# One cross-attention and expert kernel: token scaling on GpSimd, and four merges around it

## What is computed

```
ln   = layer_norm(x) * ln_w + ln_b                 # per token
xq_j = fp8(bf16(clip(ln / in_scale_j)))            # j = q, qx, k, v: four scalings of the same tokens
q    = LN(xq_q @ wq) * qln_w + qln_b               # LN over each head's 128 columns; k likewise, v without LN
core = softmax(q k^T / sqrt(128)) v                # 8 groups, 2 heads each, 64 keys
xout = the same with qx, and with kx, vx from the context
catq = fp8(bf16(clip([core, xout] / proj_smooth)))
x    = x + catq @ wproj * scale
x    = x + experts(layer_norm(x))                  # 8 experts, top 2, and a shared one
```

## Time and profile before

| | us |
|---|---|
| median of 3 runs | 955.73 |
| lowest, highest | 955.66, 956.96 |
| the profiled execution | 956.31 |
| its span | 954.5 |

### The profile page before, as it was taken

The page is one execution under the profiler, slowest core; times in us unless marked ns, Lnnn a source line. Parts: engine busy times, 40 slices in busy tenths (PEclk is TensorE's granted clock), DMA queues, the critical chain, the costliest instruction groups (busy, mean ns, idle before and its releaser), DMA issues.

```text
span 954.5 us, 23599 instructions
## 1 busy us (share of the span) xinstructions
PE 916.9 (96%) x8264; PEld 621.1 (65%) x8264; DVE 793.8 (83%) x1720; ACT 735.6 (77%) x1370; POOL 454.5 (48%) x673
## 2 busy tenths in 40 slices
PE   5688999999999999999999999999999999999997
PEld 3365666766767676766767667666655566666665
DVE  6889999999999999999999999987998744444443
ACT  5998899899899899899999999864656545555554
POOL 5335656465565555555555555531056513333333
PEclk9989999999999999999999999999999999999999
DMA  9933201001001001001100100213558713333323
GB/s 215 333 90 70 64 24 51 30 30 44 29 30 46 29 29 46 29 30 31 44 30 24 52 29 24 102 44 117 178 157 262 249 48 54 51 74 51 46 32 37
DMA packets 36754, 70.48 MB, mean 74 GB/s; under 512 B 3616, under 2 KB 24736, under 8 KB 36512
## 3 DMA queue, kind: packets, MB, share of 16 engines
q1 hardware_dynamic: 27184, 54.39, 17.5%
q0 software_dynamic: 9456, 14.59, 9.1%
HBM read 55.52 MB, written 18.68 MB: 78 GB/s over the span
## 4 chain that ended last, share of the span: by engine, by line
PE 64%; DVE 21%; issue 7%; ACT 5%; POOL 1%; DMA 1%; DVEq 0%; POOLq 0%; ACTq 0%
PE b_pj L346 17%; PE b_tr L362 7%; PE b_pj L1339 5%; PE b_o L403 5%; PE b_o L1374 5%; PE b_sc L374 4%; PE b_acc L446 4%; PE b_o L1466 3%; PE b_tr L1339 3%; DVE ssq L526 3%; PE b_sc L1339 3%; DVE nrm L537 3%; PE b_pj L1419 2%; DVE cat L578 2%; PE b_pt L1363 2%
## 5 line engine op out<-in xcount | busy, mean ns | idle before, releaser
L700 POOL TENSOR_TENSOR root<-vareps,neghalf 128x4 f32<-128x4 f32 (+1 forms) x128 | 173.8, 1358 | 10.0
L693 POOL TENSOR_TENSOR var<-ssq,unit 128x4 f32<-128x4 f32 (+1 forms) x128 | 54.3, 424 | 235.1 <-DVE ssq L526 235.1
L346 PE MATMUL b_pj<-w_hi,xq 128*128 128x512 f16 x384 | 148.9, 388 | 1.1 <-DVE xq L682 0.8
L346 PE MATMUL b_pj<-w_lo,xq 128*128 128x512 f16 x384 | 148.3, 386 | 0.0
L526 DVE TENSOR_REDUCE ssq<-sq 128x4 f32<-128x512 f32 x192 | 130.3, 679 | 3.3 <-ACT sq L458 2.1
L537 DVE TENSOR_TENSOR nrm<-raw,rstd 128x512 f32<-128x512 f32 x192 | 128.8, 671 | 4.2 <-POOL rstd L704 3.5
L362 PE MATMUL b_tr<-ident,nrm 128*128 128x128 f32 x768 | 120.5, 280 | 11.6 <-DVE nrm L537 7.0
L458 ACT ACTIVATE sq<-b_pj 128x512 f32<-128x512 f32 x192 | 114.2, 595 | 18.2 <-PE b_pj L346 14.7
L1315 POOL DMA_INDIRECT out<-xn x39 | 60.6, 1553 | 136.2 <-ACT xn L1545 110.5
L362 PEld LDWEIGHTS b_tr<-ident,nrm 128*128 128x128 f32 x768 | 87.7, 141 | 48.3 <-DVE nrm L537 18.1
L468 ACT ACTIVATE raw<-b_pj 128x512 f32<-128x512 f32 x192 | 116.0, 604 | 0.0
(11 more groups left out here) (327 smaller groups left out, 2271.7 us busy)
## 6 DMA issues: line engine op xcount, KB each, us to landing
nst<-in_ffw SPq DMA_DIRECT2D x40, 512.0 KB, 3.3
wload<-in_ffw SPq DMA_DIRECT2D x20, 512.0 KB, 4.5
xbuf<-zero SPq DMA_DIRECT2D x13, 387.0 KB, 9.6
xn<-xbuf SPq DMA_DIRECT2D x9, 516.0 KB, 3.7
x_sb<-in_x SPq DMA_DIRECT2D x4, 512.0 KB, 14.1
wproj<-in_ctxT SPq DMA_DIRECT2D x1, 2048.0 KB, 10.9
xhl<-in_w_all SPq DMA_DIRECT2D x4, 512.0 KB, 18.2
wproj<-in_wprojT POOLq DMA_DIRECT2D x4, 512.0 KB, 5.0
```

Source lines behind the costliest of these rows:

```text
L346: last = pe.matmul(o, x, w[kind][:, k, at:at + BANK], start=(k == 0 and n_ == 0), stop=(k == KT - 1 and n_ == len(terms) - 1))
L700: pool.tensor_tensor(root[:, r % 2, c, :], vareps[:, r % 2, c, :], neghalf[:, 0:1].unsqueeze(2).to_broadcast(shape), ALU.pow).then_inc(s[" ...
```

## The change

Five edits.

1. From tile 2 on, the four scalings of a tile are one GpSimd product `y16 = lnT * rin` of 128x1024 elements with both inputs in SBUF. It stands behind both rstd chains and the rows in GpSimd's list, in the second of the four iterations of a tile. ScalarE's eight instructions for that tile go. `y16` now holds all four parts.
2. VectorE clips and rounds a tile's tokens in two instructions of 128x1024 instead of eight of 128x256, in the third of the four iterations.
3. The rstd chain is two instructions: one with a multiply and an add, and the power. The factor `unit` moves into the eviction's scale, as `hw = weight * unit`, two small VectorE instructions at the start.
4. `b_o0` and `b_o1` are one tensor `b_oo`, and `cat` is one instruction over both banks (128x1024).
5. The squares of banks 1 and 2 are summed in one instruction, behind `cat`; `sq` has three buffers instead of two.

```diff
             def act_square(c):
-                    after(act, "ssq_done", m - 1)
-                    act.activation(sq[:, m % 2, :], b_pj[c % 2][:, :], ACT.Square)
+                    after(act, "ssq_done", 2 * N if c else 2 * N - 1)
+                    act.activation(sq[:, c, :], b_pj[c % 2][:, :], ACT.Square)
...
+            def pool_token_scaled(pool, t, part):
+                if part != 1:
+                    return
+                pool.wait_ge(s["lnt_done"], KT * t + KT)
+                pool.wait_ge(s["q16_done"], scaled(t))
+                pool.tensor_tensor(y16[:, :, :, :], lnT[:, :, :].unsqueeze(2).to_broadcast([P, KT, 4, P]),
+                                   rin[:, :, :].rearrange("p j k -> p k j").unsqueeze(3).to_broadcast([P, KT, 4, P]),
+                                   ALU.mult).then_inc(s["y_done"], 1)
...
             def dve_quantize(dve, t, part):
+                if t >= 2 and part != 2:
+                    return
+                j = slice(0, 4) if t >= 2 else PARTS[part]
...
-                last = dve.tensor_tensor(cat16[:, :, b * S:(b + 1) * S], ...    # for b in range(2)
+                dve.tensor_tensor(cat16[:, :, :].rearrange("p a (b s) -> p b a s", s=S),
+                                  b_oo[:, :, :].rearrange("p b (a s) -> p b a s", s=S), smooth, ALU.mult)
...
             def pool_rstd(q):
-                    pool.tensor_tensor(var, ssq, unit2, ALU.mult)
-                    pool.tensor_tensor(vareps, var, epsc, ALU.add)
-                    pool.tensor_tensor(root, vareps, neghalf, ALU.pow)
-                    pool.tensor_tensor(rstd, root, unit, ALU.mult)
+                    pool.tensor_scalar(vareps, ssq, unit2[:, j:j + 1], EPS, ALU.mult, ALU.add)
+                    pool.tensor_tensor(rstd, vareps, neghalf, ALU.pow)
...
-                    (PREP, act_token_scaled, "tokens"),
...
-                    (3, dve_squares(0), "squares 0"),
+                    (3, dve_squares(0, 1), "squares 0"),
                     (1, dve_sum, "sum"),
-                    (3, dve_squares(1), "squares 1"),
                     (-1, dve_cat, "cat"),
-                    (3, dve_squares(2), "squares 2"),
+                    (3, dve_squares(1, NN), "squares 1"),
...
-                run_slots(pool, [(3, pool_rstd(0)), (3, pool_rstd(1)), (ROWS, pool_rows)],
+                run_slots(pool, [(3, pool_rstd(0)), (3, pool_rstd(1)), (ROWS, pool_rows), (PREP, pool_token_scaled)],
```

More of the change, by code:

```diff
@@ L205, in build @@
             b_sc = bank("b_sc", banks)
-            b_o = [bank(f"b_o{n}", banks) for n in range(2)]
+            b_oo = banks.enter_context(nc.psum_tensor("b_oo", [P, 2, BANK], F32))
+            b_o = [b_oo[:, n, :] for n in range(2)]
             b_acc = bank("b_acc", banks)
@@ L576, in dve_cat @@
                 after(dve, "clip_done", N)
[L577 to L581, removed]
+                smooth = wide(rsm[:, r * n:(r + 1) * n], S).unsqueeze(1).to_broadcast([P, 2, n, S])
+                dve.tensor_tensor(cat16[:, :, :].rearrange("p a (b s) -> p b a s", s=S),
+                                  b_oo[:, :, :].rearrange("p b (a s) -> p b a s", s=S), smooth, ALU.mult)\
+                    .then_inc(s["cev_done"], 1)
             def dve_clip(dve, N):
@@ L634, in act_token @@
                 act.wait_ge(s["tr_done"], t + 1)
-                after(act, "y_done", 4 * t)
+                after(act, "y_done", scaled(t))
                 for k in range(KT):
@@ L691, in step @@
                     shape = [P, (NN - 1) if q else 1, HC]
[L692 to L698, removed]
+                    pool.wait_ge(s["ssq_done"], 2 * N + (2 if q else 1))
+                    pool.tensor_scalar(vareps[:, r % 2, c, :], ssq[:, r % 2, c, :], unit2[:, j:j + 1], EPS,
+                                       ALU.mult, ALU.add).then_inc(s["pool_ve"], 1)
                     pool.wait_ge(s["pool_ve"], e)
-                    pool.tensor_tensor(root[:, r % 2, c, :], vareps[:, r % 2, c, :],
-                                       neghalf[:, 0:1].unsqueeze(2).to_broadcast(shape), ALU.pow).then_inc(s["pool_pw"], 1)
-                    pool.wait_ge(s["pool_pw"], e)
                     after(pool, "norm_done", NN * (N - 2) + (NN if q else 1))
-                    pool.tensor_tensor(rstd[:, r % 2, c, :], root[:, r % 2, c, :],
-                                       unit[:, j:j + 1].unsqueeze(2).to_broadcast(shape), ALU.mult)\
+                    pool.tensor_tensor(rstd[:, r % 2, c, :], vareps[:, r % 2, c, :],
+                                       neghalf[:, 0:1].unsqueeze(2).to_broadcast(shape), ALU.pow)\
                         .then_inc(s["rs_done"], 1)
@@ L860, in attention_scalar @@
                     (-2, "raw 3"): lambda: high(2, 4),
-                    (-2, "token"): lambda: (high(2, 5), squares(0)),
-                    (-2, "tokens"): lambda: (squares(1), high(3, 2), squares(2)),
+                    (-2, "token"): lambda: (high(2, 5), squares(0), squares(1), high(3, 2), squares(2)),
                     (-2, "rows"): lambda: (high(3, 3), squares(3)),
@@ L1592, in _ @@
                 for n in range(2, 6):
[L1593 removed]
+                    tail[FIRST - 2 + n, "token"] = shared(n)
                 attention_scalar(act, tail)
```

59 lines of the change are left out of this document (32 added, 27 removed).

## The result

The changed kernel takes 972.19 us (median of 4 runs, 970.95 to 976.32) against 955.72: a ratio of 1.0177 with the interval 1.0164 to 1.0191. It is slower by 16.5 us; the forecast was 947 and its range ended at 972.

What follows compares the result with a forecast made beforehand. TensorE was taken as full in the regular attention, late behind VectorE by 2%, with a ceiling near 19 us; 956.3 - 7.2 - 2.0 - 0.5 + 0.2 = 946.8, stated as 947 us, range 943 to 972.

Steps and rivals of the forecast that it cites:

- The step that failed: GpSimd's product beside VectorE's nrm: VectorE's loss put at nothing; the other end was the product's whole length.
- the second half of such an instruction holds nobody: Read from L720, GpSimd's 256 elements of 1.23 us: a nrm begun in its middle took 0.69 us, no more than others.
- Rival 1: GpSimd's product holds the critical nrm: 1.6 us in each of 14 tiles, +22, less 6 gained, 972; chance 0.33.
- a gain of 6 us: In rival 1, what remains of the gain from the first stretch and a part of the waits: -6 us.
- Rival 2: nrm starts first, the product holds bank 2's nrm: TensorE loses some 0.5 us per tile; 953 to 956; chance 0.14.
- The waits of 9.6 us: Transposes' weight loads waiting for nrm, 110 to 600 us: ceiling 9.6 us there, three quarters to go, -7.2 us.
- That floor: Regular stretch: behind the waits for nrm TensorE's own instructions follow one another, so relieving other engines gives no more.
- rival 3: TensorE is full already: 3 to 4 of the 9.6 us go at most, 951 to 954; chance 0.11.
- The chain: GpSimd's rstd chain for banks 1 and 2: no fourth step, rstd ready at 313.74 instead of 314.37, 0.63 us earlier.
- The first slots: First 110 us, seven to eight slots with VectorE late: -2 us, bounds 0 and -5, of 8.0 us of waits.
- the place of the joined sums: VectorE's merged sums of squares: their place costs nothing, as the chain for banks 1 and 2 already waited for both.
- ScalarE's saved time: Eight instructions, 3.1 us per tile, go: worth nothing in the regular stretch, some tenths in the first slots; ScalarE near 85%.

Runs made afterwards that it cites:

- e8: The changed kernel with the GpSimd product replaced by a multiply of one tensor with one factor per partition, same place and size; 956.17 us in one run.
- e3: The changed kernel with the GpSimd product moved ahead of bank 0's rstd, waiting for the iteration's last nrm (bank 2); 955.80 us, ratio 0.9998 to the kernel before.
- e9: The changed kernel with the product one iteration later, ahead of bank 0's rstd, waiting only for bank 1's nrm; 957.06 us, ratio 1.0000 to the kernel before.
- e7: e3 with edit 5 undone (sums of squares of banks 1 and 2 apart again); 952.28 us, ratio 0.9948 to the kernel before.
- e1: The changed kernel with edits 1 and 2 undone, ScalarE writing the scaled tokens again; 960.67 us, ratio 1.0044 to the kernel before.
- e5: The kernel before with edit 3 alone, the shorter rstd chain; 956.60 us, ratio 1.0000 to the kernel before.
- e6: The kernel before with edit 5 alone, the joined sums of squares; 960.54 us, ratio 1.0051 to the kernel before.
- e11: The kernel before with edits 1 and 2 only, the product placed as in e3; 957.56 us, ratio 1.0012 to the kernel before.

## Why the prediction was wrong

**The step that failed** is the one that put VectorE's loss at nothing, on the earlier trace rows; measured, the held `nrm` costs 1.1 us in each of 14 tiles, 15.7 us. The rows were true: a `nrm` begun 0.62 us into GpSimd's 256 elements was not held. What I made of them was not. I took "the second half of such an instruction holds nobody" for a price of the whole product, though the `nrm` at stake begins 0.1 to 0.2 us behind the product, in its first part, which those rows do not show. e8 shows what they did show: a GpSimd instruction of one tensor and factors per partition lets VectorE go long before it ends. A product with two inputs holds it almost to its end: 1.90 us, and `nrm` ends 0.55 us behind it.

The Trainium skill (SBUF — State Buffer, Who interferes with whom) had named the mechanism, and this trace agrees with it on the product (0.69 us became 2.38). I set its rule aside with one counterexample; the counterexample narrowed the rule and did not refute it. Where the Trainium skill (SBUF — State Buffer, Terms) has the shared ports "held for the full instruction", e8 disagrees: 3.38 us long, and a two-input `nrm` that began inside it ended 1.2 us before it did. The 4497 ns that the Trainium skill (GPSIMD Engine Reference, section 3.1) gives for 2048 elements are of an add; half of it, an estimate of 2.25 us, is above the 1.90 measured for this product.

**Rival 1** was the right one. Its product of 2.5 us was 1.90, its `nrm` came 0.07 us behind the product where 0.1 to 0.2 was worked out, and the stall by its own formula is then 1.0 us per tile; measured is 37.41 against 36.29 per four in e3, 1.12 us per tile, 15.7 us over 14. It named 972 us, and that it met 972.19 is partly luck: two errors of some 6 us cancel. The stall was 22 us and is 16, and it counted a gain of 6 us where e3, with nobody held, has none (955.80); with a product of 1.9 us it would have said some 964. **Rival 2** did not come about, as `nrm` stood behind the product. Its cost was tried as e9: held in the second place, the norm costs nothing in the regular stretch, where I had put 0.5 us.

**The waits of 9.6 us** were mis-sized as a ceiling. They are waits of the weight loads, which idle beside running matmuls. The matmuls' own wait for `nrm` is a line of its own in the view of the earlier trace rows, which I had said was not there. That line, and then what weight loads still wait in e3 and in e7 (110 to 600 us):

```profile
PE b_tr L362 <- DVE nrm L537: 1.3, 2, 1.0
```

```profile
PEld b_tr L367 <- DVE nrm L543: 5.5, 14, 1.8
```

```profile
PEld b_tr L367 <- DVE nrm L545: 1.5, 1, 1.5
```

e3 and e7 both take 36.29 per four: the waits by which they differ cost no time. With VectorE's delay out of the way (e3, e7) four slots shrink by 0.29 us, 36.58 to 36.29, which is 3.7 us over slots 9 to 56 (439.2 to 435.5), not 7.2. It all lies in one slot of four, which takes 8.6 to 8.7 us instead of 8.9; the other three take 9.59, 9.37 and 8.72 in either kernel. It comes with edits 1 and 2, as every kernel that has them shows it and e1, e5 and e6 do not. From there on TensorE's own instructions set the pace: in e7 its matmuls wait 1.1 us of 490 for `nrm`, in one place, and for no other engine. That floor was the forecast's, and rival 3 had its size right with 3 to 4 us.

**The chain** gained 0.3 us and not 0.63. In the changed kernel it goes from 317.19 to 320.19, 3.00 us, before from 311.06 to 314.37, 3.31. What it gained is the fourth step. The multiply-add lasts until `prob` ends (1.23 us), where I had let it end with `nrm`. That alone moves nothing, as I had let the power wait for `prob`. The power starts 0.14 us behind `prob`'s end in both kernels and takes 1.69 us (1.70 before). I had counted its end 1.49 us behind `prob`'s; the 1.49 us are from the clip's end, and from `prob`'s it was 1.84 us before, too.

**The first slots** were put at -2 us and the place of the joined sums at nothing. e6 has +4.2 us for that edit (960.54 against the 956.30 of the runs beside it), 2.8 of it in slots 1 to 8. I had said that the chain for banks 1 and 2 waited for both sums before, too; true, but bank 1's sum used to run while VectorE waited for the last square, and the join moved its 0.6 us behind the wait. In the regular stretch this is nearly covered (e6 has 0.1 us more per four, e3 none more than e7), in the stretches where other work delays the squares it is not. There TensorE's granted clock is at half for longer, too, which the forecast did not have at all: 1.2 us of the 2.8 (see e6).

Right were: the product's length is no problem for GpSimd at its old place; ScalarE's saved time (41.99 of 50 us, 84%, against 46.66; 85% was forecast); and that this saved time is worth little, as TensorE is full. VectorE's is hidden in the changed kernel, as its 47.94 of 50 us (48.67 before) hold the stretched `nrm`; in e3, with none held, it is 464.75 of the 490 us from 110 to 600, against 474.14 before, 95% where 94% was forecast.

## What to carry to other kernels

Before work goes to GpSimd, find what VectorE runs in the window: an instruction with both inputs in SBUF that starts behind a GpSimd one can stand still for most of its length, and work out whom the held one feeds; here the same product costs 16 us ahead of one `nrm`, nothing beside sums and PSUM work. A row in which two instructions overlap unharmed prices only the part in which they overlapped. And joining two instructions is not free where their inputs come one after the other: the first one's time moves behind the second one's wait. Where TensorE waits longer for it, read the granted clock of the next stretch, too.

## What was not expected of the hardware

GpSimd's multiply of 1024 elements by one factor per partition takes 3.42 us on average, the product of two tensors of the same size 1.90 us. GpSimd's multiply-add of 8 elements takes 1.23 us beside VectorE's two instructions with two SBUF inputs each, and 0.28 us in the four places of the changed kernel where VectorE runs none such. What remains open: why the multiply with one factor lets a `nrm` go first that begins 0.05 us behind it, where the product does not; and the time behind slot 64's first scores, which differs by up to 1.7 us between kernels that are alike there (322.4 us before, 324.0 in e11). In e5's profiled execution, the longest of its eleven (961.34 us; the median is 956.60), it is 328.2 us, with the clock at half for 3.4 us at 749 us, where no other trace has it.
